# The last stage before the second layer's experts: normalising on ScalarE, and routing dealt out between the blocks two groups later

## The reference

```
h2 = relu(gcn_conv(h1, W2, b2, src, dst, n))      # agg of 64 numbers a node, W2 64 x 256
x  = x + h2 + mix(xn)                             # residual
h  = layernorm(x)
logits = h @ gate_w + gate_b                      # 8 experts
idx = argmax(softmax(logits));  prb = its probability
pos = (cumsum(one_hot(idx)) * one_hot(idx)).sum(-1) - 1
buf[idx, pos] = h   where pos < capacity          # then the experts run on buf
```

## Time and profile before

| what | us |
|---|---|
| median of the 3 runs | 5247.54 (5239.28 to 5250.59) |
| the profiled execution | 5253.34 |
| its span in the trace | 5251.4 |
| the stage in it | about 161 |

### The profile page before, as it was taken

How to read it: one execution, slowest core, us unless ns; L and a number is a source line. 1 busy time by engine, 2 the same in 40 slices (tenths; PEclk the granted TensorE clock), 3 DMA queues, 4 the chain that set the end, 5 groups by cost and what they waited for, 6 DMA issues and landing times. The chain is left out here.

```text
span 5251.4 us, 62217 instructions
## 1 busy us (share of the span) xinstructions
PE 3522.0 (67%) x13908; PEld 2764.9 (53%) x13909; DVE 2526.5 (48%) x5949; ACT 1049.5 (20%) x2215; POOL 3048.2 (58%) x2894
## 2 busy tenths in 40 slices
PE   4866666665399975999655555554555555567998
PEld 3734444433277765888544444443444545455665
DVE  5477777777712553222643444444333333463444
ACT  0122222221199911332100000000000000042111
POOL 1177777777299944222277777776777777722111
PEclk9976677777699987999565666665555555567999
DMA  5398777777588863222511111112111111132221
GB/s 111 115 248 247 241 241 241 241 241 224 158 264 272 272 210 112 70 70 62 166 33 32 33 33 33 33 32 44 33 32 33 33 33 33 30 118 89 73 79 34
DMA packets 437408, 616.97 MB, mean 117 GB/s; under 512 B 104714, under 2 KB 315466, under 8 KB 437003
## 3 DMA queue, kind: packets, MB, share of 16 engines
q1 hardware_dynamic: 306767, 391.02, 23.6%
q0 software_dynamic: 107728, 200.97, 15.6%
q10 hardware_dynamic: 22812, 23.86, 1.7%
HBM read 418.38 MB, written 211.62 MB: 120 GB/s over the span
## 5 line engine op out<-in xcount | busy, mean ns | idle before, releaser
L1886 POOL DMA_INDIRECT big<-t_d,src_tiles x1564 | 1482.6, 948 | 622.9 <-issue 457.3
L2109 PE MATMUL v_bank<-big,v_oh 128*128 x3328 | 685.2, 392 | 914.5 <-POOLq L1882 855.5
L2109 PEld LDWEIGHTS v_bank<-big,v_oh 128*128 128x128 f32 x3328 | 651.8, 300 | 990.9 <-issue 990.8
L704 POOL DMA_INDIRECT big<-xl_d,src_steps x832 | 794.1, 954 | 261.0 <-issue 230.2
L815 PE MATMUL se_z_ps<-big,se_oht 128*128 x1664 | 687.7, 569 | 370.9 <-DVE se_z L744 326.5
L1964 DVE TENSOR_TENSOR big<-big,v_bank 128x64 f32 x1664 | 366.8, 220 | 1138.9 <-PE v_bank L2109 917.5
L815 PEld LDWEIGHTS se_z_ps<-big,se_oht 128*128 128x128 f32 x1664 | 424.2, 276 | 634.1 <-issue 555.2
L1134 POOL TENSOR_TENSOR ae_v<-ae_v,ex 128x2048 f32<-128x2048 f32 x104 | 380.6, 3673 | 109.8 <-DMA ae_v<-xj_d 108.7
L744 DVE TENSOR_TENSOR se_z<-se_z_ps,big 128x528 f32<-128x528 f32 x416 | 291.7, 701 | 279.9 <-DMA big<-xl_d,src_steps 268.7
L1176 PE MATMUL ae_sums<-ae_v,ae_oh 128*128 128x266 f32 x1664 | 396.2, 395 | 25.9 <-ACT ae_oh L1125 17.3
L1176 PEld LDWEIGHTS ae_sums<-ae_v,ae_oh 128*128 128x128 f32 x1664 | 309.1, 191 | 112.9 <-issue 60.7
(11 more groups left out here) (480 smaller groups left out, 4926.0 us busy)
## 6 DMA issues: line engine op xcount, KB each, us to landing
xj_d<-big SPq DMA_DIRECT2D x208, 528.0 KB, 3.3
ae_v<-xj_d SPq DMA_DIRECT2D x208, 528.0 KB
se_dlb<-dlr_d SPq DMA_DIRECT2D x104, 256.0 KB, 5.1
big<-t_d,src_tiles POOLq DMA_INDIRECT x1564
buf_d<-ne_blank SPq DMA_DIRECT2D x4, 4112.0 KB
e_xs<-buf_d SPq DMA_DIRECT2D x56, 258.0 KB, 2.9
big<-xl_d,src_steps POOLq DMA_INDIRECT x832
cp_y<-y_d SPq DMA_DIRECT2D x14, 896.0 KB, 7.3
```

Source lines behind the costliest of these rows:

```text
L704: nc.gpsimd.indirect_dma_start(half_of(u)[:, k, :], None, table, bass.IndirectOffsetOnAxis(ap=m.src[:, t:t + 1], axis=0)).then_inc(landed[ ...
L1886: nc.gpsimd.indirect_dma_start(rows[:, t % RING, :], None, table, bass.IndirectOffsetOnAxis(ap=m.srct[:, t:t + 1], axis=0)).then_inc(lande ...
L2109: last = nc.tensor.matmul(bank[u][:, k * MH:(k + 1) * MH], oh[:, u, k, :], of_block(rows, at[k]), start=True, stop=True)
```

## The change

Three things are done.

1. In `edge_steps` the key table is no longer `fd` itself: POOL works out `(fl - clamp(fl, 0, 127)) * 8192 + fd` in four operations of 128 x 896 numbers after its gathers, and SP stores that, as its last transfer of the stage. The wait for the store moves from the head of VectorE's list in `project_nodes` to the end of SP's.
2. The weights of the last stage are loaded in `convolve(1)`, by SP, ahead of its block loads; tiles for them are allocated outside. VectorE clears one of these tiles first.
3. In the stage, `scale` works on a whole group in one instruction, two groups ahead; `normalise` leaves VectorE only the reciprocal, the token column and one short instruction `shift = -mean * rstd`, and ScalarE does the seven normalising activations `rstd * x + shift`; `choose` and `place` of group g-2 become generators whose instructions are dealt out between the blocks of group g (three after each of the first three blocks, four after each later one); the ranking products and the exponential stand after the third block; `disp` holds three groups of rows.

```
 # edge_steps, POOL, after its gathers
+ pool.wait_ge(floats, 3)
+ nc.gpsimd.tensor_scalar(inside, fl, 0.0, float(P - 1), ALU.max, ALU.min).then_inc(told, 1)
...
+ nc.gpsimd.tensor_tensor(runs, fl, inside, ALU.subtract).then_inc(told, 1)
...
+ nc.gpsimd.tensor_scalar(runs, runs, 8192.0, None, ALU.mult).then_inc(told, 1)
...
+ nc.gpsimd.tensor_tensor(runs, runs, fd, ALU.add).then_inc(told, 1)
 # edge_steps, SP, at its end
+ sp.wait_ge(told, 4)
+ sp.dma_start(m.key_d.rearrange("(j p) e -> p j e", p=P), runs[:, :, :]).then_inc(m.keyed, 16)
 # project_nodes
  (DVE)  - dve.wait_ge(m.keyed, 16)
  (SP)   + sp.wait_ge(m.keyed, 16)
 # convolve(1): SP, before load(k)
+ sp.wait_ge(s["emptied"], 1)
+ sp.dma_start(m.last_w2[0:MH, :], a["L1_gnn_W2"]).then_inc(s["later"], 16)
...                                                 (b2, gate_w, gate_b likewise)
 # finish_and_route1: DVE
- V.tensor_scalar(us[:, k % 4, 0:MH], m.agg[:, k, :], m.dinv[:, k:k + 1], None, ALU.mult)
+ V.tensor_tensor(us[:, g % 2, :, 0:MH], m.agg[:, part, :], m.dinv[:, part]...to_broadcast([P, G, MH]), ALU.mult)
- for i in range(G):
-     V.tensor_scalar(disp[:, g % 2, i, 0:D], rows_of(k), m.mean[:, k:k + 1], m.rstd[:, k:k + 1], ALU.subtract, ALU.mult)
+ V.scalar_tensor_tensor(shift[:, part], m.mean[:, part], -1.0, m.rstd[:, part], ALU.mult, ALU.mult).then_inc(s["shifted"], 1)
+ for g in range(NGR + 2):
+     first = choose(g - 2) if g >= 2 else iter(())
+     second = place(g - 2) if g >= 2 else iter(())
+     for i in range(G):
+         if g < NGR:
+             finish(G * g + i)
+             if i > 0:
+                 stats(G * g + i - 1)
+         for _ in range(3 if i < CHOSEN else 4):
+             next(first if i < CHOSEN else second, None)
...
+     if g < NGR:
+         stats(G * g + G - 1)
+         variance(g)
+         if g + 2 < NGR:
+             scale(g + 2)
+         normalise(g)
 # ACT
+ def normal(g):
+     act.wait_ge(s["shifted"], g + 1)
+     if g >= DG:
+         act.wait_ge(sent[g % DG], 16 * G * (g // DG))
+     for i in range(G):
+         nc.scalar.activation(disp[g % DG][:, i, 0:D], rows_of(k), ACT.Identity, bias=shift[:, k:k + 1], scale=m.rstd[:, k:k + 1])
  # per k: turned(k + 4), normal_turned(k - G), residual(k - G); after the third: exp of g - 2; per group: Sqrt of g, normal(g)
 # PE
- pe.wait_ge(s["weights"], 64)
  # per k: turn(k + 4), project(k + 1), turn_normal(k - G), gate(k - G - 1); after the third: rank(g - 2)
```

More of the change, by code:

```diff
@@ L1924, in _ @@
                 pipeline(sp, NB, 1, (0, load))
+                if which == 1:
+                    sp.wait_ge(s["later"], 64)
                 if which == 0:
@@ L1933, in _ @@
                 V = nc.vector
+                if which == 1:
+                    V.memset(m.last_w2[:, :], 0.0).then_inc(s["emptied"], 1)
                 V.tensor_copy(iota, m.iota[:, :]).then_inc(s["started"], 1)
@@ L2194, in finish_and_route1 @@
         bank = [ctx.enter_context(nc.psum_tensor(f"fr_bank{i}", [P, 512], F32)) for i in range(8)]
[L2195 to L2198, removed]
+        s = {n: m.sem("fr_" + n) for n in ("masks ones u_ready ut_made ut_ready made res_ready stat chain var std xn_ready "
+                                           "xt_made xt_ready g_made g_back l_in exped counted totals t_ready p_ready r_ready slots shifted "
+                                           "sent0 sent1 sent2 experts res_out").split()}
+        sent = [s["sent0"], s["sent1"], s["sent2"]]
         def rows_of(k):
@@ L2264, in _, with scale @@
                 V = nc.vector
[L2265 to L2273, removed]
+                V.memset(us[:, :, :, MH:P], 0.0).then_inc(s["ones"], 1)
+                dve.wait_ge(s["ones"], 1)
+                V.memset(us[:, :, :, MH], 1.0).then_inc(s["ones"], 1)
+                def scale(g):
+                    part = slice(G * g, G * g + G)
+                    if g >= 2:
+                        dve.wait_ge(s["ut_made"], G * (g - 1))
+                    V.tensor_tensor(us[:, g % 2, :, 0:MH], m.agg[:, part, :], m.dinv[:, part].unsqueeze(2).to_broadcast([P, G, MH]),
+                                    ALU.mult).then_inc(s["u_ready"], 1)
                 def finish(k):
@@ L2359, in place @@
                     V.tensor_tensor(m.slots[:, 0, part], sf[:, :], absent[:, part], ALU.add).then_inc(s["slots"], 1)
+                    yield
                     c.sync()
[L2361 to L2364 removed]
+                    V.tensor_copy(disp[g % DG][:, :, RW - 2], m.prob[:, part]).then_inc(s["p_ready"], 1)
+                scale(0)
+                scale(1)
                 dve.wait_ge(s["masks"], 10)
                 c.did(V.tensor_scalar(absent[:, :], valid[:, :], -1.0, -1.0e6, ALU.add, ALU.mult))
[L2367 to L2374 removed]
+                for g in range(NGR + 2):
[8 more added lines that the diff above has]
+                            next(first if i < CHOSEN else second, None)
+                        if i == CHOSEN - 1:
+                            for _ in first:
+                                pass
+                    for _ in second:
+                        pass
+                    if g < NGR:
                         stats(G * g + G - 1)
                         variance(g)
[L2377 to L2379 removed]
+                        if g + 2 < NGR:
+                            scale(g + 2)
                         normalise(g)
[L2381 to L2382 removed]
             @block.scalar
@@ L2465, in _, with rank @@
                 project(0)
-                for g in range(NGR + 1):
+                def rank(g):
+                    pe.wait_ge(s["counted"], g + 1)
+                    if g >= 2:
+                        pe.wait_ge(s["slots"], g - 1)
+                    flat = mask[:, :, :].rearrange("p b e -> p (b e)")
+                    nc.tensor.matmul(ranks(g), tri[:, :], flat, start=True, stop=True)
+                    nc.tensor.matmul(totals(g), m.ones[:, :], flat, start=True, stop=True).then_inc(s["totals"], 1)
+                for g in range(NGR + 2):
                     for k in range(G * g, G * g + G):
@@ L2475, in _ @@
                                 gate(k - G - 1)
[L2476 removed]
+                        if g >= 2 and k % G == CHOSEN - 1:
+                            rank(g - 2)
+                    if 1 <= g <= NGR:
                         gate(G * g - 1)
[L2478 to L2483 removed]
 def weights1(m):
@@ L2733, in build @@
         end_stage(nc, m)
-        for which in range(2):
-            convolve(nc, m, a, which)
+        convolve(nc, m, a, 0)
+        end_stage(nc, m)
+        with ExitStack() as last:
+            m.last_w2 = last.enter_context(nc.sbuf_tensor("last_w2", [P, D], F32))
+            m.last_wg = last.enter_context(nc.sbuf_tensor("last_wg", [P, KC, NE], F32))
+            m.last_bg = last.enter_context(nc.sbuf_tensor("last_bg", [P, NE], F32))
+            convolve(nc, m, a, 1)
             end_stage(nc, m)
-        finish_and_route1(nc, m, a)
+            finish_and_route1(nc, m, a)
         experts1(nc, m, a)
```

112 lines of the change are left out of this document (64 added, 48 removed).

## The result

The changed kernel takes 5254.56 us (median of 20 runs) against 5247.96 before (20 runs): a ratio of 1.0014, 95% interval 1.0008 to 1.0019, so some 6.6 us slower where 12.4 us less was forecast. That is outside the forecast range at its upper end, and of the other sign; it is small, but its interval leaves out no change. The profiled execution is a long one, 5267.95 us with a span of 5266.2; its parts are compared here, not its total. Two executions of later runs were slow ones and are left out of the times, one of e11 and one of e10 (6878.69 us), which is also e10's profiled one, so that only the durations of its gathers are read from it.

What follows compares the result with a forecast made beforehand. TensorE with two stalls a group was taken as the bound; -3.0 - 0.5 - 12.0 + 2.8 + 0.3 = -12.4 us gave 5240.9 against the profiled 5253.34, 5235 beside the median; range 5217 to 5251.

Steps and rivals of the forecast that it cites:

- The five periods: Last stage's steady group periods: each saves 4.9 us of old stalls less 2.5 of new; -12.0 in five, bounds -4.5 to -19.5.
- the new waits: TensorE's group-start stalls for the first normalised row (1.9 or 0 us) and first copy-out (2.1 or 1.0); 2.5 taken together.
- The old waits: TensorE's waits for scale (3.1 us a group) and of ranking products for choose (1.8); together 4.9 a group, to vanish.
- The second rival: Last stage: stalls only moved, clock low throughout, periods 19.7 to 20.1 us; gain 1 to 2, total 5247; chance 0.24.
- The first rival: Last stage: clock stays high throughout, period 14.1 us, 30.5 saved in five, total 5216; chance 0.12.
- The front: First stage's end: four POOL key operations of 1.6 us each, ending at 81.4, then the store; +0.3 us, bounds 0 to +2.
- The third rival: First stage: POOL's key operations held up beside VectorE, 7.66 us each, +24 there, net +12, total 5259; chance 0.07.
- the start: Last stage's start: TensorE's first turn earlier with weights already loaded, -3.0 us (-2 to -4); first group -0.5.
- the weights hidden in the convolution: Graph convolution: four more SP transfers ahead of the first block load vanish in 18 us of cover; 0 us.
- the tail: Last stage's end: copy behind activations +2.1, exponential's table load +1.5, rows not behind choose -0.8; +2.8 us, bounds 0 to +4.
- the seven activations: ScalarE's normalising of a group's rows in the last stage: seven at 0.47 us, 3.3 us in all.
- The second group: Last stage's second group: no choose in front before, and keeps a stall of the new kind; 0 us.

Runs made afterwards that it cites:

- e11: Kernel without the key-table part, rows turned ten blocks late, four row buffers, the remaining group wait filled with five unread products; 0.9901 of the kernel before.
- e10: Kernel before with only the key-table change, its arithmetic in three VectorE operations and POOL's list untouched; ratio 1.0006 to the kernel before.
- e1: Kernel before with only the key-table change, by four POOL operations; ratio 1.0026, 12.5 us slower than the kernel before.
- e7: Kernel before with only the key-table change's four POOL operations, each on one column, the key table staying old; ratio 1.0014, 6.4 us slower.
- e9: Kernel before with only the last stage's weights loaded in the graph convolution; ratio 0.9993 to the kernel before, 2.8 us by the medians.
- e5: Changed kernel without the key-table part, TensorE making six unread products in each of its two group-start waits; ratio 0.9921 to the kernel before.
- e6: Changed kernel without the key-table part, rows turned ten blocks late, four row buffers, no normalising step waiting for scatters; 0.9914 of the kernel before, 5202.6 us.
- e3: Changed kernel without the key-table part, TensorE's first turn of a group waiting for all seven rows; 0.9984 of the kernel before.

## Why the prediction was wrong

Wrong in sign, by two steps of its sum.

1. *The five periods* (-12.0). The step that failed is "a period saves 4.9 - 2.5": it holds TensorE's own 15.3 us fixed. The waits went about as forecast, from 27.2 us in five to 12.4, so 14.8 less. But TensorE's work grew by 12.3, from 73.33 to 85.59, because the clock fell from 0.67 to 0.58. That leaves -2.5 (101.1 before, 98.6 after), outside the term's own bounds of -4.5 and -19.5. The 2.5 a period for the new waits was taken halfway between the two clocks, and it came out because the first of them begins at the high clock (1.9 reckoned, 1.55 measured) and the second lies in the low one (1.0 and 0.97). The old waits were 5.4 a period and not 4.9. The second rival named the clock ("stalls only moved", 0.24) and met the periods' length; it took a low clock as a chance, not as a consequence of the two waits that the forecast had just costed, and its evidence was thin: TensorE is busy for 12.77 of the tail's 30.80 us. The first rival had the right size for a kernel at the high clock and the wrong condition: the "two stalls of 2 us a group" that it counts against itself are what kept the clock down, so they did not leave a part of the gain but took nearly all. Open is why two short waits leave a lower clock than the old longer ones did.
2. *The front* (+0.3, measured +5.0, +7.0 in e1). "One takes 1.6 us" scaled one row by columns; the four took 3.64, 2.09, 2.47 and 2.07, with their handovers 10.5. Even the 6.4 that was forecast ended at 81.4 with the store still to come, so the reckoning had no slack. The third rival's sign came (86.95, later than 84) but not its price of 7.66 an operation, and its point from which it decides (4.9) counted on a gain in the periods that was not there: that the kernel is slower does not bear out its mechanism.
3. *Missing:* the gathers. That they change with POOL's list is shown by e7 and e10; the +4.3 is an estimate from their medians.
4. *Right:* the start (-3.0 and -0.5 forecast, -3.5 measured); the weights hidden in the convolution (e9's gathers and first blocks unchanged); the tail (+2.8, measured +2.6, but its three terms were not measured one by one, so this may be luck); the seven activations (3.3 forecast, 3.55 measured). The second group was +2.3 and not 0, for the reason of point 1.

The Trainium skill, ScalarE: Activation LUTs, What ACT_TABLE_LOAD costs, has pointer operands at about 93 ns each: by the estimate worked out from it a row in a series takes 0.49. The trace agrees: one activation takes 0.59 and seven 3.55, and (3.55 - 0.59) / 6 = 0.49.

The Trainium skill, TensorE: Matmul & The Clock Gate, HAM oscillation — how this bites in real kernels, tells of a kernel whose waits send it back to the low clock before each piece of work, so that the way up is paid every time. The traces here agree, and show it for a wait of 1.55 us.

## What to carry to other kernels

Before a wait of TensorE is costed by its length, read the granted clock just before and after it: if the clock falls at the waits, shortening them can be worth little, and removing them, or filling them with products that nobody reads, can be worth far more than their length (here some 35 us, where the waits of five periods were 12.4). Four instructions put into an engine's list early can cost in the steady loops behind them; where a loop of a thousand gathers sets the pace, compare its median before and after any edit of that engine's list. And work moved under a barrier is hidden only if the chain's last step, store included, ends before it.

## What the runs showed of the hardware

- TensorE's clock fell in a wait of 1.55 us and stayed at 0.50 for the 16.6 us behind it, in which a second wait of 0.97 lies (the changed kernel); a wait of 0.7 between filled stretches did not bring it down (e5, 1.00 throughout), and a single one of 1.15 did in two groups of four (e6).
- A kernel that waits longer can be as fast: 21.2 us of waits in five periods against 12.4, 2.5 us less in all (e3).
- Four small instructions on POOL changed 832 later gathers from 954 to 946 ns and 1564 others from 945 to 952.
- Four dependent operations of 128x896 on POOL took 2.07 to 3.64 us each.
